# Graph network of four layers: twenty small bf16 products after each tick of the third layer, into a bank that nothing reads

## The reference

```python
edge_index = jnp.stack([src, dst])
x = _layernorm(x + _L0_gnn_ref(x, edge_index, edge_attr_64, ...))    # attention over edges (GAT)
x = _layernorm(x + _L1_gnn_ref(x, edge_attr_128, edge_index, ...))   # filters made of edge features ("cf")
x = _layernorm(x + _L2_gnn_ref(x, edge_index, W, b))                 # degree-normalised sum ("gcn")
x = _layernorm(x + _L3_gnn_ref(x, edge_index, W1, b1, W2, b2))       # sum, then two dense maps ("gin")

def _L2_gnn_ref(x, edge_index, W, b):
    h = x @ W.T
    src, dst = (with one loop per node)
    deg = segment_sum(ones, dst, N); dinv = rsqrt(deg)
    msgs = h[src] * (dinv[src] * dinv[dst])[:, None]
    return segment_sum(msgs, dst, N) + b
```

## Time and profile before

| | us |
|---|---|
| median of 3 runs | 5716.53 (5711.46 to 5719.04) |
| the profiled execution | 5724.69 |
| its span, first to last instruction | 5723.0 |
| mean granted TensorE clock, share of 2.4 GHz | 0.656 |
| gathers of the attention stage | 103.6 to 1444.5 |
| gathers of "cf" | 2029.4 to 3212.6 |
| gathers of "gcn" | 3278.7 to 4458.0 |
| gathers of "gin" | 4497.6 to 5677.3 |

### The profile page before, as it was taken

One profiled execution on the slowest core, in us unless ns is written; L12 is line 12 of the kernel. 1 busy time (PEld: TensorE's weight loads), 2 busy tenths in 40 slices (PEclk: granted clock), 3 DMA queues, 4 the chain that ended last, 5 costly groups with the idle time before them and its releaser, 6 DMA issues.

```text
span 5723.0 us, 55777 instructions
## 1 busy us (share of the span) xinstructions
PE 2659.1 (46%) x13337; PEld 2162.5 (38%) x13337; DVE 2751.9 (48%) x7464; ACT 1432.0 (25%) x4291; POOL 3543.8 (62%) x3833
## 2 busy tenths in 40 slices
PE   2667676666688823333333323333333223333334
PEld 2455555555466623333333313222323223233333
DVE  5688777776788823333333313333333323333333
ACT  2686565555566610000000100000000000000000
POOL 2566666566255566766666366666666566666664
PEclk8898888888777755666655655555555555555555
DMA  6566655565277721111111111111111111111111
GB/s 140 139 155 149 143 142 144 138 144 133 65 226 225 224 77 48 49 50 48 50 49 50 29 48 49 49 48 51 48 51 48 40 47 48 48 52 47 51 48 38
DMA packets 433196, 490.28 MB, mean 86 GB/s; under 512 B 88331, under 2 KB 335327, under 8 KB 432870
## 3 DMA queue, kind: packets, MB, share of 16 engines
q0 software_dynamic: 131904, 288.49, 19.4%
q1 hardware_dynamic: 296424, 194.27, 12.7%
q10 hardware_dynamic: 4542, 3.90, 0.3%
HBM read 359.63 MB, written 126.70 MB: 85 GB/s over the span
## 4 chain that ended last, share of the span: by engine, by line
another core or an unknown queue 31%; DVE 13%; issue 10%; PE 6%; DVEq 4%; ACT 0%; DMA 0%; POOL 0%; ACTq 0%; SPq 0%; POOLq 0%
DVE acc L979 10%; PE bank L1763 5%; DVEq L754 2%; DVEq L751 1%; DVE arena L1019 1%; PE bank L1700 1%; DVE stats L995 1%; DVEq L987 0%; DVE x_sb L943 0%; PE bank L1695 0%; PE bank L1742 0%; DVE moments L998 0%; DVE arena L1081 0%; DVE acc L1031 0%
## 5 line engine op out<-in xcount | busy, mean ns | idle before, releaser
L1784 POOL DMA_INDIRECT arena<-node_table,pick x1664 | 1613.8, 970 | 851.0 <-issue 482.4
L1763 PE MATMUL bank<-arena 128*128 128x128 f32 x4992 | 1145.9, 402 | 2100.3 <-DVE arena L1019 1584.0
L979 DVE TENSOR_TENSOR acc<-acc,bank 128x128 f32 x2496 | 719.0, 288 | 2437.6 <-remote 1855.3
L1763 PEld LDWEIGHTS bank<-arena 128*128 128x128 f32 x4992 | 998.1, 297 | 2263.3 <-DVE arena L1019 1693.2
L1784 POOL DMA_INDIRECT arena<-gat_table,pick x832 | 849.5, 1021 | 511.9 <-issue 221.7
L1784 POOL DMA_INDIRECT arena<-message_table,pick x832 | 808.1, 971 | 377.6 <-issue 240.6
L1019 DVE TENSOR_TENSOR arena<-iota_free,local 128x512 f32<-128x512 f32 x624 | 430.6, 690 | 0.5
L1358 ACT ACTIVATE rstd<-moments,eps_col 128x4 f32<-128x4 f32 (+2 forms) x39 | 11.6, 297 | 1600.4 <-issue 827.6
L1377 ACT COPY arena<-acc 128x128 f32 x98 | 22.1, 294 | 1479.8 <-DVE acc L979 1479.8
L1689 PE MATMUL bank<-arena 128*128 x1664 | 332.6, 362 | 41.4 <-DVE arena L1095 33.3
L1689 PEld LDWEIGHTS bank<-arena 128*128 128x128 f32 x1664 | 284.6, 258 | 109.1 <-issue 109.1
(11 more groups left out here) (263 smaller groups left out, 3640.3 us busy)
## 6 DMA issues: line engine op xcount, KB each, us to landing
message_table<-arena POOLq DMA_DIRECT2D x208, 256.0 KB, 3.3
filter_table<-arena SPq DMA_DIRECT2D x196, 256.0 KB
arena<-filter_table SPq DMA_DIRECT2D x624, 64.0 KB
xt<-edge_cols SPq DMA_DIRECT2D x131, 256.0 KB
arena<-local_rows SPq DMA_DIRECT2D x208, 128.0 KB
arena<-node_table,pick POOLq DMA_INDIRECT x1664
arena<-edge_cols SPq DMA_DIRECT2D x65, 256.0 KB
arena<-gat_table,pick POOLq DMA_INDIRECT x832
```

Of the source, the lines that this page charges most:

```text
L979: e.tensor_tensor(a, a, bank[6 + t % 2][:, s * P:(s + 1) * P], ALU.add).then_inc(sums, 1)
L1763: ins = e.matmul(bank[6 + n % 2][:, s * P:(s + 1) * P], hot[n % 2][:, s, :], gathered[:, slot(n, s), 0:D], start=True, stop=True)
L1784: e.indirect_dma_start(out=dst, out_offset=None, in_=table, in_offset=bass.IndirectOffsetOnAxis(ap=index, axis=0)).then_inc(done, 16)
```

## The change

After the four products of each tick of "gcn", TensorE issues 20 matmuls of `hot_copy` with itself, bf16, 128 by 128, into the first 128 columns of bank 0. Nothing reads this bank in that layer, and the matmuls increment no semaphore; `plain_product` is incremented by the last real product, ahead of them. Since "cf" still uses bank 0 in its `finish_second`, TensorE first waits until all 13 sets of `n2_rows` are there. "cf" and "gin" call `plain_layer` without a fill.

```diff
+BUSY = 20
...
+            def no_work():
+                pass
+
+            def busy_work():
+
+                for _ in range(BUSY):
+                    e.matmul(bank[0][:, 0:P], hot_copy[:, :], hot_copy[:, :], start=True, stop=True)
+
-            def plain_layer(layer, base, finish):
+            def plain_layer(layer, base, finish, fill=no_work):
                 for n in range(TICKS + AFTER):
...
                     ins.then_inc(plain_product, 1)
+                    fill()
...
             plain_layer("cf", 0, finish_second)
-            plain_layer("gcn", TICKS, no_finish)
+            e.wait_ge(n2_rows, NS)
+            plain_layer("gcn", TICKS, no_finish, busy_work)
```

## The result

The changed kernel took 5742.13 us in the median of five runs (5726.28 to 5750.45), the kernel before 5716.53 us in five. The ratio is 1.0051, with a 95% interval of 1.0034 to 1.0068: 0.5% slower, 19 to 39 us. The medians alone are 25.6 us apart. The forecast was 5783 us, 66 us more. The sign is right and the time lies in the range, but the size is more than twice what was measured.

The account below looks back on a forecast made before the run. Bound: GpSimd's 129.7 us of stops on a full ring, as unbroken indirect gathers hold back TensorE's completions. Terms 0 + 6 + 60 = 66 us on the 5716.53 us median gave 5783 us; range 5690 to 5900, 8 times in 10.

Parts of the forecast that it names:

- The wait on `n2_rows`: Before the third layer's first product: TensorE's wait for the second layer's last rows costs 0, since the first gather comes later.
- The direct time: Third layer's 20 products a tick: 1.8 us at the high clock, 3.0 at the low; 6 us after the last gather.
- The holds term: Third layer: the fill's 8320 added instructions beside gathers cost 60 us, chosen among 10, 49 and 121 us.
- Faster: Third layer: a busy TensorE is not held back, stops end; 5593 us, or 5658 with half gone; chance 0.16.
- Slower by far: Third layer: holds grow with the instructions; at two ticks a stop 188 us more, 5905 us; chance 0.17.
- No difference: Third layer: holds stay as they are, TensorE catches up, the fill costs 0 to 10 us; 5717 to 5730; chance 0.17.
- The change does not do what it says: Third layer: TensorE idles in holds, clock little above 0.54; forecast's time, up to 31 us at the end; no separate chance.
- (1): Second and fourth layer keep 1183 and 1180 us between first and last gather.
- (2): Third layer: 4160 matmuls on the new line, 0.09 us apart at the high clock; clock above 0.54.
- (3): Third layer: GpSimd's "remote" waits rise from 129.7 to about 190 us, by number more than by length.
- (4): Third layer: in catching-up ticks the sums stand 3 us or more apart.
- (5): Ring's first filling in the third layer: sums still come tens of microseconds after their products' records.

Follow-up runs that it names:

- the narrow products: Changed kernel with its 20 products a tick cut from 128 to 6 columns: 5741.59 us with holds, kernel before 5720.56; without holds 5058.34 and 5069.58.
- the run with few records: Changed kernel without fill; third layer has one bf16 128 x 512 product and one of four sums a tick: 5670.19 us, kernel before 5720.67.

## Why the prediction was right and wrong

**The bound** was read rightly: GpSimd's stops for a full ring, caused by late completions and not by TensorE's work. With holds, taking both engines' records away removed the stops (4.5 us), and without holds the stops are absent with all the work in place. The reading that it is TensorE's completions that are late was too narrow: VectorE's instructions are held in the same way.

**The wait on `n2_rows`, 0.** Right as far as it can be told: the two kernels with holds and without fill show no cost, and in the changed kernel TensorE's wait before its first product is 12.2 us with the gather as what ended it, as long as before.

**The direct time.** Sized too large. The 20 products were put at 1.8 us at the high clock; the trace after has them in 1.28:

```profile
4465.26 1.28 PE L1760 MATMUL bank<-arena 128*128 128x128 bf16 x20
4466.39 1.16 PE L1772 MATMUL bank<-arena 128*128 128x128 f32 x8
...
4468.57 1.16 PE L1772 MATMUL bank<-arena 128*128 128x128 f32 x8
```

Product and fill together are 2.18 us, from product to product, about what VectorE's sums and mask take (2.1 us a tick). So the tail grew by 1.2 us, not 6. The nearest row was that of the 6-column matmuls, 0.037 us each, and not the f32 record: 0.056 us was measured.

**The holds term, 60.** This is the step that failed, by a factor of two: it measured 30.2 us. Its mechanism stands (number of instructions beside gathers, as many again with 40), the price per instruction does not: 7.2 ns were taken and 3.7 measured. The bounds of 1.2 and 5.9 ns from the plain layers held it; what pulled the value above both was the attention stage's 14.5 ns, called "nearest in amount". In the execution of the changed kernel without holds that stage is 1162 us long against 1053 to 1063 of the plain layers, with no stop in these: so about 100 of the 161.6 us that were divided among its instructions are there without any holds. A second weakness: the 5.9 ns came from 3.9 us between two layers, while the second layer's stretch less the fourth's lies between -9.6 and 8.1 us in ten executions with holds (1.6 in the changed kernel's). A difference of 3.9 us carries hardly a price at all.

**The rivals.** *Faster* fell: the clock rose to 0.70, and 0.89 with 40 products, and the layer grew all the same. The Trainium skill's "TensorE: Matmul & The Clock Gate", section "HAM oscillation — how this bites in real kernels", asks for a TensorE without idle gaps. The product did get faster, 2.08 to 1.16 us, but nothing waited for its length. *Slower by far* had the arithmetic right and one factor wrong: at 2.5 ticks a stop (208 / 83) it expected stops of 3.0 us each, and they shrank to 2.0. *No difference* is what happens wherever completions are not held (1.0015), which the forecast had not as a case: it took the holds for a property of the kernel on this chip. *The change does not do what it says* fell with the clock of 0.70.

**The signs.** (1) 1182.1 and 1180.5 us: right. (2) 4160 matmuls, the clock at 0.70: right; 0.056 us apart and not 0.09. (3) The stops went from 129.7 to 165.9 us, not to 190, by number: right in kind. (4) Sums in catching-up ticks 3 us or more apart: wrong, most of them come after 2.1 to 2.7 us as before. (5) Sums tens of microseconds late at the first filling: right, 58.8 us. (6) 38 us from last gather to last sum: it was 32.9.

## What to carry to other kernels

When a ring is full although the engine that empties it is mostly idle, look at how far apart its records start, and at the other engines' too: an even spacing (here 1.40 us) means that what costs is the number of instructions, and then fewer and wider ones cost less at the same work (11.0 against 30.4 us), and warming TensorE with small products is no remedy. Price such a term from a pair of stretches that differ in nothing else, and check first how well their difference repeats. And run the kernel before beside every experiment: here its own time moved by 650 us from set to set, and with it the whole bound.

## What the runs showed of the hardware

**Engines held to an even gait.** With holds, TensorE's and VectorE's instructions come to start 1.40 us apart while GpSimd issues indirect gathers back to back, and TensorE's 0.70 us apart some us after GpSimd has stopped, until the backlog is gone. Two records a tick on both engines do not fall behind; 5 on VectorE or 16 on TensorE do. What sits in between is open. It is not TensorE's clock or its columns (the narrow products), and not the fetching of instructions (no packet in 75 us of holds). The Trainium skill's "NOTIFIC — Programmer's Manual", section "8.4 Tracing", says that the records written for each instruction can be costly to the link to the host, and its section "1.1 The problem" that an engine never blocks on the host for them. A gait per record whatever its work would fit a path for such records that pushes back. The two sections do not settle it, and no run here tests it: every run of this case has a span and a clock read from such records, so it is open whether the kernel would have its holds without them.

**The same kernel, 650 us apart.** The kernel before takes 5062 to 5078 us in four sets and 5716 to 5758 in the first comparison and four sets. In the traces kept, the unchanged plain layers are 1041 to 1065 or 1178 to 1191 us long and the attention stage 1159 to 1165 or 1318 to 1348. The number that the runs give for the chip does not tell which: number 7 stands on a set of either kind. The same program ran either way, so it is not the program that decides; what does is open.

**A mask and a gather.** A gather's instruction on GpSimd that starts while VectorE's mask of 128 x 512 runs takes 1.28 instead of 0.95 us (177 of 184 such gathers in the run with few records took over 1.0 us, 63 of 88 in the kernel before). The Trainium skill's "SBUF — State Buffer", section "SBUF: two separate sides", names a port pair that VectorE and GpSimd share as an exclusive lock; the row agrees with such a thing. The same section's rule that TensorE never waits on anyone speaks of ports, and whatever held TensorE here for 1.40 us a record is not covered by it.

No kernel that computes the whole layer beat the kernel before by more than the scatter (without holds single runs lay up to 15 us under it, and its own thirteen runs beside one set span 28 us). The runs say where one would have to start with holds: fewer instructions a tick on both engines (with 2 and 2 the layer was 52.7 us under its neighbours' mean), which for the real work means fewer and wider sums; that was not built.
